# Two attention stages of a fused transformer kernel: constant rows cleared as 32-bit words, low-rank weights made one stage earlier, operands of the full stage copied inside SBUF

## The reference

```
x = x + 0.5 * L0_ffn(norm(x))    # A: coupled FFN, three cycles
x = x + L0_attn(norm(x))         # B: causal attention, 16 heads of 8, then its own layernorm
x = x + 0.5 * L0_ffn(norm(x))    # C: as A
x = x + 0.5 * L1_ffn(norm(x))    # D: 8 experts, top 2, and a shared one
x = x + L1_attn(norm(x))         # E: full attention, 16 heads of 8, q and v through a low-rank addition
x = x + 0.5 * L1_ffn(norm(x))    # F: as D
```

```
qkv = x @ w_qkv + b_qkv                       # then split into 16 heads of 8
q = q + (q @ a_q) @ b_q * LORA_SCALE          # per head
v = v + (v @ a_v) @ b_v * LORA_SCALE
attn = softmax(q k^T * ATTN_SCALE)            # each row of attn sums to 1
return (attn v) @ w_proj + b_proj
```

## Time and profile before

| | |
|---|---|
| median of 3 runs | 1643.41 us (1641.65 to 1648.79) |
| the profiled execution | 1641.26 us, its span 1639.3 us |
| stage A, from its first product to the end of its block | 28.34 to 115.21 us |
| stage B, causal attention, first product to last addition | 130.31 to 611.48 us |
| stage E, full attention, first product to last addition | 805.69 to 1539.94 us |
| granted PE clock, mean | 0.915 of full speed |

### The profile page before, as it was taken

The page is one execution under the profiler, slowest core; times in us unless marked ns, Lnnn a source line. Parts: engine busy times, 40 slices in busy tenths (PEclk is TensorE's granted clock), DMA queues, the critical chain, the costliest instruction groups (busy, mean ns, idle before and its releaser), DMA issues. The chain is left out here.

```text
span 1639.3 us, 30480 instructions
## 1 busy us (share of the span) xinstructions
PE 1385.8 (85%) x12316; PEld 515.1 (31%) x12316; DVE 1142.6 (70%) x1273; ACT 1033.9 (63%) x2018; POOL 154.5 (9%) x293
## 2 busy tenths in 40 slices
PE   5714899999999986679879989999999999998788
PEld 2202433333333353143432222222222222222633
DVE  2614777888888714644568889999999999994343
ACT  2402577787788833421317888888888888888121
POOL 5980100000000000000000000000000000000000
PEclk9857999999999977869858999999999999999679
DMA  2004300000000000000040110000000000000000
GB/s 74 16 0 114 122 15 5 12 4 4 10 3 4 4 9 1 1 0 0 23 113 22 42 40 5 10 3 3 3 11 3 3 3 10 3 3 3 9 0 26
DMA packets 32156, 30.26 MB, mean 18 GB/s; under 512 B 12144, under 2 KB 29200, under 8 KB 31760
## 3 DMA queue, kind: packets, MB, share of 16 engines
q1 hardware_dynamic: 32016, 28.32, 6.4%
HBM read 18.40 MB, written 9.70 MB: 17 GB/s over the span
## 5 line engine op out<-in xcount | busy, mean ns | idle before, releaser
L1018 DVE TENSOR_REDUCE ea_blockmax<-ps 128x2 f32<-128x1024 f32 x512 | 591.0, 1218 | 72.7 <-PE ps L821 72.7
L968 ACT ACTIVATE ea_prob<-ps 128x512 f32<-128x512 f32 x1024 | 547.9, 601 | 45.4 <-PE ps L854 40.0
L1018 DVE TENSOR_REDUCE ba_blockmax<-ps 128x2 f32<-128x1024 f32 (+2 forms) x320 | 325.9, 1061 | 87.8 <-PE ps L821 47.3
L821 PE MATMUL ps<-k_k_all,k_q_all 64*128 64x512 bf16 (+3 forms) x1664 | 321.4, 384 | 69.0 <-DVE ea_blockmax L1018 26.1
L968 ACT ACTIVATE ba_prob<-ps 128x512 f32<-128x512 f32 (+3 forms) x640 | 302.2, 536 | 67.5 <-PE ps L862 31.0
L883 PE MATMUL ps<-ea_prob,k_v_op 128*16 128x256 f32 x4096 | 314.7, 385 | 0.1
L854 PE MATMUL ps<-ea_q_max,k_k_all 64*128 64x512 bf16 x1024 | 217.2, 380 | 7.3 <-ACT ea_prob L968 6.5
L821 PEld LDWEIGHTS ps<-k_k_all,k_q_all 64*128 64x128 bf16 x1664 | 79.7, 93 | 383.7 <-issue 179.8
L883 PE MATMUL ps<-ba_prob,k_v_op 128*16 128x256 f32 (+1 forms) x2304 | 186.5, 372 | 0.0
L854 PE MATMUL ps<-ba_q_max,k_k_all 64*128 64x512 bf16 (+3 forms) x640 | 129.0, 351 | 6.9 <-ACT ba_prob L968 6.7
L854 PEld LDWEIGHTS ps<-ea_q_max,k_k_all 64*128 64x128 bf16 x1024 | 89.6, 94 | 81.6 <-ACT ea_prob L968 44.1
(11 more groups left out here) (265 smaller groups left out, 1245.7 us busy)
## 6 DMA issues: line engine op xcount, KB each, us to landing
ba_parts<-ba_part SPq DMA_DIRECT2D x8, 384.0 KB, 3.5
k_k_all<-ba_parts SPq DMA_DIRECT2D x48, 64.0 KB
k_q_all<-ba_parts SPq DMA_DIRECT2D x48, 64.0 KB
ea_parts<-ea_part SPq DMA_DIRECT2D x8, 384.0 KB, 3.1
k_k_all<-ea_parts SPq DMA_DIRECT2D x96, 32.0 KB
k_q_all<-ea_parts SPq DMA_DIRECT2D x96, 32.0 KB
ba_sums<-ba_pv SPq DMA_DIRECT2D x128, 9.0 KB
ea_sums<-ea_pv SPq DMA_DIRECT2D x128, 9.0 KB
```

The lines of the kernel that those rows point to most:

```text
L821: mm = pe.matmul(ps[:, MX + 2 * (u % 2) + j, 0:width], q_all[head, pair, q0:q0 + TW], k_all[head, pair, CW * kc:CW * kc + width], start=Tr ...
L968: nc.scalar.activation(prob[:, e % NP, q0:CW], ps[:, e % ST, q0:CW], ACT.Exp, scale=SCALE)\
L1018: nc.vector.tensor_reduce(blockmax[:, m % plan.AHEAD, qt, :, kc], ps[:, MX + 2 * (u % 2):MX + 2 * (u % 2) + 2, 0:width], AX.X, ALU.max)\
```

## The change

Four things are changed.

1. The six clearing and ones instructions on POOL go over the same bytes as fp32, 8192 elements a partition; the ones are written as the 32-bit word that holds two bf16 ones.
2. `bd`, `wl` and the biases are made at the end of the preparation of stage B (`if not lora`), after PE has its v and before its first fill, in PSUM banks 0 to 3. E begins at once with its items.
3. The bias of v is no longer added to v. Since the rows of the softmax sum to 1, it passes the attention unchanged: `bias_o = w_proj^T bias_v + b_proj` takes the place of `b_proj`. 16 products with ones fall away in E.
4. In E the parts no longer go to DRAM. The loads read `part` in SBUF, 8 rows a DMA. Pair 0 is loaded in halves of 1024 columns: its front half of k by SP and of q by ACT (12 DMAs each), once four items are done; its back half of k by SP once all eight are, then pairs 1 and 2, then the back half of q. E's fills go through all four query tiles of one key chunk before the next key chunk, and PE waits for the back halves where they are first read.

```diff
-                            pool.memset(k[op][HALF * j + MAXROW:HALF * j + HALF, :, :], 0.0).then_inc(cleared, 1)
+                            pool.memset(k[op][HALF * j + MAXROW:HALF * j + HALF, :, :].bitcast(fp32), 0.0).then_inc(cleared, 1)
...
-                        pool.memset(k["k_all"][HALF * j + MAXROW:HALF * j + MAXROW + 3, :, :], 1.0).then_inc(cleared, 1)
+                        pool.memset(k["k_all"][HALF * j + MAXROW:HALF * j + MAXROW + 3, :, :].bitcast(fp32), TWO_ONES).then_inc(cleared, 1)
...
-            return [(q, j, CW) for q in range(TPC) for j in range(NC)]
+            return [(q, j, CW) for j in range(NC) for q in range(TPC)]
...
+        def load_pair(queue, w, pair, cols, sem):
+
+            op, rows = ((q_all, Q_ROWS), (k_all, K_ROWS))[w]
+            for j in range(2):
+                row = 2 * HD * pair + HD * j
                 for p, firsts in rows.items():
                     for r in firsts:
                         lo = HALF * j + r
...
-                            row = 2 * HD * g + HD * j
-                            queue.dma_start(op[lo:lo + HD, g, :], parts_dram[w, p, row:row + HD, :]).then_inc(sem[g], 16)
+                        queue.dma_start(op[lo:lo + HD, pair, cols], part[row:row + HD, w, p, cols]).then_inc(sem, 16)
...
-                    mm = pe.matmul(out, tile(xn, t), weight_v, start=True, stop=not lora)
-                    if lora:
-                        mm = pe.matmul(out, k["ones"][:, :], bias_v[:, :], start=False, stop=True)
+                    mm = pe.matmul(out, tile(xn, t), weight_v, start=True, stop=True)
...
+                    if not causal and m == 0 and (kc, qt) == (NC // 2, 0):
+                        pe.wait_ge(k_back, LOADED)
+                    if not causal and (m, f) == (PAIRS * NC // 2, 0):
+                        pe.wait_ge(q_back, LOADED)
...
                 pe.wait_ge(rest_ready, len(items))
                 pe.wait_ge(v_ready, NC)
+                if not lora:
+                    for b, (name, a_t, b_m, _) in enumerate(lora_parts):
+                        for u in range(2):
+                            mm = pe.matmul(ps[:, b, 0:P], k[a_t][:, u, :], k[b_m][:, u, :], start=(u == 0), stop=(u == 1))
+                        mm.then_inc(bd_mm, 1)
+                    for b, (name, _, _, w_t) in enumerate(lora_parts):
+                        pe.wait_ge(bd_ready, b + 1)
+                        pe.matmul(ps[:, 2, P * b:P * b + P], k[w_t][:, :], bd[name][:, :], start=True, stop=True)
+                        pe.matmul(ps[:, 3, b:b + 1], bd[name][:, :], k["b" + name + "1"][:, :], start=True, stop=True)\
+                            .then_inc(w_mm, 1)
+                    pe.wait_ge(bias_ready, 2)
+                    pe.matmul(ps[:, 3, 2:3], k["wproj1"][:, :], k["bias_v"][:, :], start=True, stop=True).then_inc(w_mm, 1)
+                    pe.wait_ge(bias_ready, 3)
...
+                    if not causal and i == NC:
+                        act.wait_ge(lo_ready, NC)
+                        load_pair(nc.scalar, 0, 0, front, q_in[0])
...
-                    for c in range(NC):
-                        sp.wait_ge(parts_sent[c], 16 * 2)
-                    for g in range(3):
-                        load_group(g)
+                    sp.wait_ge(lo_ready, NC)
+                    load_pair(sp, 1, 0, front, k_in[0])
+                    sp.wait_ge(lo_ready, 2 * NC)
+                    load_pair(sp, 1, 0, back, k_back)
+                    for pair in (1, 2):
+                        load_pair(sp, 1, pair, slice(0, N), k_in[pair])
+                        load_pair(sp, 0, pair, slice(0, N), q_in[pair])
+                    load_pair(sp, 0, 0, back, q_back)
...
                     if not causal and m + 3 < PAIRS:
-                        load_group(m + 3)
+                        load_pair(sp, 1, m + 3, slice(0, N), k_in[m + 3])
+                        load_pair(sp, 0, m + 3, slice(0, N), q_in[m + 3])
```

More of the change, by code:

```diff
@@ L48 @@
 HALF_CW = CW // 2
+TWO_ONES = float(np.array([0x3F803F80], np.uint32).view(np.float32)[0])
 EXPERTS = 8
@@ L135, in load_constants @@
     k["hide_k"] = n.sb("hide_k", [P, 2, TW], bf16)
+    k["bd"] = {name: n.sb("bd" + name, [P, P], fp32) for name in "qv"}
+    k["wl"] = {name: n.sb("wl" + name, [P, P], fp32) for name in "qv"}
+    k["bias_q"], k["bias_v"], k["bias_o"] = (n.sb(name, [P, 1], fp32) for name in ("bias_q", "bias_v", "bias_o"))
     k["maxparts"] = n.sb("maxparts", [P, TPC, P], bf16)
@@ L717, in attention @@
         rest, num = k["sq"], k["cen"]
[L719 to L722, removed]
+        bd, wl, bias = k["bd"], k["wl"], (k["bias_q"], k["bk1"])
         part = n.sb("part", [P, 2, 3, N], bf16)
@@ L750, in attention @@
         LOADED = 16 * 2 * 6
+        front, back = slice(0, N // 2), slice(N // 2, N)
         def group(m):
@@ L754, in group, with load_chunk @@
             return c if causal else pair
-        def load_parts(queue, w, g):
+        def load_chunk(queue, w, c):
             op, rows, sem = ((q_all, Q_ROWS, q_in), (k_all, K_ROWS, k_in))[w]
+            cols = slice(CW * c, CW * c + CW)
             for j in range(2):
+                for p, firsts in rows.items():
+                    source = parts_dram[w, p].rearrange("(a j d) n -> j d a n", j=2, d=HD)[j, :, :, cols]
+                    for r in firsts:
+                        lo = HALF * j + r
+                        queue.dma_start(op[lo:lo + HD, :, cols], source).then_inc(sem[c], 16)
+        def load_pair(queue, w, pair, cols, sem):
+            op, rows = ((q_all, Q_ROWS), (k_all, K_ROWS))[w]
+            for j in range(2):
+                row = 2 * HD * pair + HD * j
                 for p, firsts in rows.items():
@@ L773, in _ @@
             def _(pe):
-                if lora:
[L775 to L784, removed]
-                        else:
-                            pe.matmul(ps[0:1, 5, 0:P], k["bv1"][:, :], bd[name][:, :], start=True, stop=True)\
-                                .then_inc(w_mm, 1)
-                    pe.wait_ge(w_ready, 4)
                 for i, (w, c) in enumerate(items):
@@ L1010, in _ @@
                         low(i - 1)
+                if not lora:
+                    for b, (name, _, _, _) in enumerate(lora_parts):
+                        dve.wait_ge(bd_mm, b + 1)
+                        nc.vector.scalar_tensor_tensor(out=bd[name][:, :], in0=ps[:, b, 0:P], scalar=LORA_SCALE,
+                                                       in1=k["ident"][:, :], op0=ALU.mult, op1=ALU.add)\
+                            .then_inc(bd_ready, 1)
+                    dve.wait_ge(w_mm, 2)
+                    for b, (name, _, _, _) in enumerate(lora_parts):
+                        nc.vector.tensor_copy(wl[name][:, :], ps[:, 2, P * b:P * b + P])
+                    for b, name in enumerate("qv"):
+                        nc.vector.tensor_copy(k["bias_" + name][:, :], ps[:, 3, b:b + 1]).then_inc(bias_ready, 1)
+                    dve.wait_ge(w_mm, 3)
+                    nc.vector.tensor_tensor(k["bias_o"][:, :], ps[:, 3, 2:3], k["bproj1"][:, :], ALU.add)\
+                        .then_inc(bias_ready, 1)
                 for kind, m, f in plan.order:
@@ L1067, in send_parts @@
                         .then_inc(parts_sent[c], 16)
-                def load_group(g):
-                    for w in (1, 0):
-                        load_parts(sp, w, g)
                 def send_sums(m):
```

33 lines of the change are left out of this document (11 added, 22 removed).

## The result

The kernel got slower: 1656.45 us median (20 runs, 1653.05 to 1667.55) against 1643.32 us (20 runs, 1635.58 to 1660.10). The ratio is **1.0091**, 95% interval 1.0071 to 1.0110; 1597 us had been predicted.

A forecast was written before the change was run, and what follows sets the result against it. No engine was full; POOL ending stage A, the start of stage E and E's window loads were taken as limits. 31.5 + 0 + 12.6 + 0 = 44.1 us off 1641.26 gave 1597 us, range 1588 to 1634.

The forecast's parts named there:

- The loads of windows 3 to 7: Stage E, behind each window's sums: loads from 8 SBUF partitions keep the DRAM loads' 0.33 us issue pace, cost 0.
- Step 1: End of stage A: 32-bit words shorten POOL's six memsets, so PE starts B at 84.03, gain 31.5 us.
- Step 2: Stage B's preparation: the added low-rank work is covered by 13.1 us before the first fill, cost 0.
- step 3: Start of stage E: PE's first item moves from 810.17 to 805.7, everything bound to it 4.5 us earlier.
- Steps 3 and 4: Start of stage E: PE's first fill begins at 826.3 instead of 838.93, gain 12.6 us.
- The bound from above: Stage E's loads: late SBUF-to-SBUF copies of 64 rows took 0.61 and 0.81 us each; set aside for their shape.
- The rates used against it: For E's loads: 98 GB/s, and 168 GB/s to 8-row SBUF destinations in stage B, taken as supporting the 0.33 us pace.
- Rival A: The SBUF source paces E's loads at 0.61 us a DMA: 40 us lost in all, 1637 us; chance 0.28.
- rival B: E's loads at 0.81 us a DMA make the kernel 27 us slower, 1668 us; chance 0.05.
- Rival C: Stage A: bytes set the pace of POOL's fill, so its 31.5 us are missing, 1629 us; chance 0.03.
- Rival D: Stage E: SBUF loads land sooner and the five waits shrink, or ACT's issues are cheap, 1588 to 1591; chance 0.10.
- The rule of the Trainium skill that was weighed: For E's loads: 27.2 GB/s a port, two ports for 8 neighbouring partitions, so 54 GB/s, 14.5 us a pair.

The follow-up runs named there:

- the last: The changed kernel with only the 120 loads of stage E's windows 3 to 7 read from DRAM, plus eight sends: 1614.8 us, ratio 0.984.
- the second: The changed kernel with all of stage E's loads put back to DRAM, on SP, with the sends as before: 1603.2 us, ratio 0.975.
- the third: The changed kernel with its SBUF-to-SBUF loads issued one window earlier, the back half of pair 0's q last: 1604.1 us, ratio 0.977.
- the probe: A program without the computation, only trains of DMAs by kind, run once: 0.68 us an issue SBUF to SBUF, 0.34 DRAM to SBUF.

## Why the prediction was wrong

The failed step is the one under "The loads of windows 3 to 7": "I take the same pace, **0**". It was +49.7 us in the profile, and some 42 to 53 in the experiments that took it away (the last, the second and the third). An issue of a copy from SBUF to SBUF takes 0.66 us on SP, not 0.33, so each pair's loads came 7.7 us late, and that outweighs everything that was right.

- *Step 1*, 31.5 us: right. POOL took 6.95 us an instruction, PE idled 9.38 us, B began at 84.02.
- *Step 2*, 0: right in B. Its other side, 4.5 us less in E, was in step 3, and showed as 5.3 us at the first fill (second experiment).
- *Steps 3 and 4*, 12.6 us: 7.5 at the first fill. The mis-sized term is ACT's twelve issues, 9.30 us where SP's 4.01 was taken; the difference of 5.3 is the whole miss (5.1). Then "pair 1 is issued to 837.1 and needed at 844.6" failed, and by SP's pace more than by ACT's: between the last low part and the end of pair 1 stand 36 of SP's issues, 24 us where 12 were taken, and PE waited 7.18 us. Of 7.5 us gained, 2.3 were left at the first sums.
- *The loads.* The bound from above was at hand: 0.61 us an issue, measured 0.66. It was set aside as "many small pieces", by the shape. For copies of few rows the probe shows that the source counts: 8 rows cost 0.68 from SBUF and 0.34 from DRAM, one row 0.62 and 0.29. But with 64 rows, as in the earlier trace rows, both are alike, 0.57 and 0.56, so that row would probably have been about as long with a source in DRAM (the probe's rows had 4 KB, those of the earlier trace rows 256 B). It told little of the source, its neighbour had 0.81, and that it lay within 8% of the right price was in good part luck. What could be said beforehand was that no row had this source with this shape, and that a term which counts five times deserved more than 0. The rates used against it were of copies from DRAM, which tell nothing of an issue from SBUF.
- *Rival A* had the mechanism and nearly the pace, yet gave 1634 to 1637. With 0.66 instead of 0.61 a pair is 8 us later instead of 6.6; and it took each us of lateness as one us of time. The runs show 10.3 for 7.7, since PE goes on at 0.50 of its clock behind a wait of 9 us. By the prediction's own arithmetic 0.66 us gives 40 us in the windows, and the start lost 10.3 of its 12.6: 44.1 - 50.3 is 6 us slower, 1647, on rival B's side of its threshold of 0.65. Five surcharges of 2.6 us make 1660, beside a median of 1656.45, which thus lies between A's 1637 and B's 1668. A and B together had a third of the chance, and B's 0.05 was too low, since its threshold of 0.65 lay between the two rows at hand, 0.61 and 0.81.
- *Rival C*, that POOL's fill gains nothing, fell: six instructions at 6.95 us.
- *Rival D*: ACT's issues weren't cheap, and even with no waits for DMAs in windows 3 to 7 there was little to gain, 2.6 us by the two kernels with DRAM loads.

The rule of the Trainium skill that was weighed (SBUF — State Buffer, "Door 1: The DMA port swizzle") gave 14.5 us for a pair, near the measured 16.0, but not for its reason: one queue reached 48.5 GB/s and took as long with a quarter of the bytes. Near its 54 GB/s came two queues on the same 8 rows, 55 GB/s here. The Trainium skill's page DMA: Bandwidth & Descriptors ("Issuing engines are not separate DMA queues") says that the sequencer's time to initiate a DMA "is usually small relative to the DMA itself". Here the issues, 0.66 us each, set the pace of the 32 KB copies; the runs of this case decide.

## What to carry to other kernels

Where one queue issues many small DMAs, count issues, not bytes. Take the time of one from a row that has both the same memories at its ends and the same number of rows: here changing the memories took 8-row copies from 0.34 to 0.68 us, and going from 8 to 64 rows took loads from DRAM from 0.34 to 0.56. Where there is no such row, let the range of the forecast span the rows that there are. A load that stands behind a step of a loop, with waits already exposed, should be moved ahead before it is made "cheaper": it cost 10.3 us a window in place and nothing one window earlier. Behind waits of 8.5 us, of 4.6 and even of 2.8 PE went on at its lower clock, so lateness cost more than its length.

## What the runs showed of the hardware

- Time of one issue of 8 rows, one queue alone, on SP: DRAM to SBUF 0.34 us, SBUF to DRAM 0.51, DRAM to DRAM 0.62, SBUF to SBUF 0.68 (0.66 with a quarter of the columns). ACT: 0.34 and 0.71. POOL: 0.52 for either source.
- SP and ACT side by side, each SBUF to SBUF from rows of its own: 0.71 and 0.73 us; from the same 8 rows, whole: 1.19 and 1.08. SP's loads from DRAM beside ACT's SBUF copies: 0.33 us for the first, then 0.66. SP beside POOL: 1.0 (with gaps of up to 2.69 us) and 0.5, rows apart or not, but 0.67 and 0.51 while SP's were halves. Why is open.
- PE's granted clock in the 6 us behind a wait of 8.49 us was 0.50; at the same place of the kernel before, behind a wait of 0.78 us, 1.00. Behind a wait of about 4.6 us it was 0.50 too, behind one of 2.83 us 0.51.
